# Second scatter: six row transfers a step in the attention instead of four

## The reference

```python
x = x + 0.5 * ffn(layernorm(x), ...)      # mixture of experts
x = x + attn(layernorm(x), ...)           # causal, 16 heads of 64
x = x + 0.5 * ffn(layernorm(x), ...)      # same weights as the first

def ffn(h):                                # h: tokens x 128
    scores = sigmoid(h @ gate_w.T)         # 64 experts, 8 groups of 8
    # the 4 best groups stay, of their experts the 8 best; weights normalised, times 2.5
    y = sum over experts e of w_dense[:, e] * ((silu(h @ Wg[e]) * (h @ Wu[e])) @ Wd[e])
    return y + (silu(h @ Ws_gate) * (h @ Ws_up)) @ Ws_down
```

## Time and profile before

| | us |
|---|---|
| median of 3 runs | 1654.45 (1654.39 to 1654.9) |
| profiled execution, its own time | 1653.0 |
| span of the profile, first to last instruction | 1651.3 |
| TensorE (PE) busy | 1571.9 (95%) |
| VectorE (DVE) busy | 1199.7 (73%) |
| ScalarE (ACT) busy | 776.2 (47%) |
| GpSimd (POOL) busy | 669.7 (41%) |
| POOL L481, both scatters, 256 transfers | 265.3, 1036 ns each |

### The profile page before, as it was taken

One profiled execution on the slowest core, in us unless ns is written; L12 is line 12 of the kernel. 1 busy time (PEld: TensorE's weight loads), 2 busy tenths in 40 slices (PEclk: granted clock), 3 DMA queues, 4 the chain that ended last, 5 costly groups with the idle time before them and its releaser, 6 DMA issues. The chain is left out here.

```text
span 1651.3 us, 27254 instructions
## 1 busy us (share of the span) xinstructions
PE 1571.9 (95%) x8683; PEld 1016.0 (62%) x8683; DVE 1199.7 (73%) x3446; ACT 776.2 (47%) x2105; POOL 669.7 (41%) x931
## 2 busy tenths in 40 slices
PE   5899999998999899999999999998989999999999
PEld 2444444445888677777777776774448986444443
DVE  4698888664555578989898988765866855768675
ACT  2334323222444577777777766773224443222222
POOL 1000288885000334333434105435880003888740
PEclk9999999999999899999999999999999999999999
DMA  9999565563666201000101001104555764666652
GB/s 183 221 261 238 135 148 123 140 144 85 171 190 186 59 22 29 23 22 21 26 20 27 8 4 40 35 25 108 136 129 147 192 189 127 147 147 143 145 131 64
DMA packets 202043, 181.31 MB, mean 110 GB/s; under 512 B 39408, under 2 KB 154288, under 8 KB 201904
## 3 DMA queue, kind: packets, MB, share of 16 engines
q1 hardware_dynamic: 175056, 132.34, 34.0%
q0 software_dynamic: 16384, 33.59, 7.6%
q10 hardware_dynamic: 10464, 13.63, 2.4%
HBM read 121.83 MB, written 57.67 MB: 109 GB/s over the span
## 5 line engine op out<-in xcount | busy, mean ns | idle before, releaser
L840 ACT ACTIVATE f_hid<-banks 128x512 f32<-128x512 f32 (+1 forms) x264 | 157.6, 597 | 506.3 <-PE banks L800 506.2
L481 POOL DMA_INDIRECT x_rows<-r_xk,r_idx x256 | 265.3, 1036 | 137.9 <-issue 53.5
L812 PE MATMUL banks<-f_hid,wd 128*128 128x512 f32 x528 | 273.3, 602 | 11.1 <-DVE f_hid L875 11.1
L862 DVE TENSOR_TENSOR f_hid<-banks,f_hid 128x512 f32<-128x512 f32 (+1 forms) x264 | 181.4, 687 | 139.6 <-ACT f_hid L840 139.2
L796 PE MATMUL banks<-r_xT_d,gu 128*128 128x512 f32 x528 | 275.0, 603 | 4.3 <-DMA wd<-in_L_ffn_We_down 2.7
L800 PE MATMUL banks<-r_xT_d,gu 128*128 128x512 f32 x528 | 272.3, 597 | 0.0
L875 DVE TENSOR_TENSOR f_hid<-f_mix_wide,f_hid 128x512 f32<-128x512 f32 x256 | 175.9, 687 | 32.4 <-DMA f_mix_wide<-mix_rows 30.0
L517 POOL DMA_INDIRECT f_g<-y_rows,r_idx x128 | 129.8, 1014 | 163.3 <-DMA y_rows<-f2q_yq 132.3
L517 POOL DMA_INDIRECT a_g<-y_rows,r_idx x128 | 125.1, 977 | 160.1 <-POOLq L1602 105.1
L812 PEld LDWEIGHTS banks<-f_hid,wd 128*128 128x128 f32 x528 | 99.6, 192 | 144.9 <-issue 119.8
L800 PEld LDWEIGHTS banks<-r_xT_d,gu 128*128 128x128 f32 x528 | 100.6, 191 | 129.2 <-issue 125.2
(11 more groups left out here) (237 smaller groups left out, 2836.4 us busy)
## 6 DMA issues: line engine op xcount, KB each, us to landing
f_mix_wide<-mix_rows SPq DMA_DIRECT2D x124, 512.0 KB, 6.9
x_rows<-zero ACTq DMA_DIRECT2D x12, 1024.0 KB, 6.8
f1q_xq<-x_rows SPq DMA_DIRECT2D x48, 256.0 KB, 3.2
y_rows<-f1q_yq SPq DMA_DIRECT2D x48, 256.0 KB, 2.4
f2q_xq<-x_rows SPq DMA_DIRECT2D x48, 256.0 KB, 3.1
y_rows<-f2q_yq SPq DMA_DIRECT2D x48, 256.0 KB, 2.4
x_rows<-r_xk,r_idx POOLq DMA_INDIRECT x256
wd<-in_L_ffn_We_down SPq DMA_DIRECT2D x7, 512.0 KB, 10.6
```

What stands on the lines that cost most here:

```text
L481: nc.gpsimd.indirect_dma_start(x_rows[:, :], bass.IndirectOffsetOnAxis(ap=b.idx[:, f, CT * k + t, j:j + 1], axis=0), b.xk[:, k, t, :], Non ...
L812: mm = nc.tensor.matmul(acc[:, :], w["wd"][0:rows, 2 * p, :], d.hid[0:rows, g % HIDS, :], start=(p == 0), stop=(p == PAIRS))
L840: nc.scalar.activation(d.hid[0:rows, g % HIDS, :], gate_bank[g % 3][0:rows, :], ACT.Silu)\
L862: nc.vector.tensor_tensor(d.hid[0:rows, g % HIDS, :], up_bank[g % 3][0:rows, :], d.hid[0:rows, g % HIDS, :], ALU.mult).then_inc(gated, 1)
```

## The change

`dispatch` takes a range of single transfers in place of a half tile. In the attention the fifteen steps 49 to 63 issue `SCATTER_STEP` = 6 transfers each in place of 4, so 90 in place of 60. `ffn_second` issues the other 38 in place of 68. There the layer norm operation `rstd_of(in_dense[0])` (L473) stands behind 12 transfers, as before. The order of the transfers and the clears behind those of `ffn_second` are as they were. The first feed-forward block's scatter is written in the new form and has the same instructions.

```diff
-        def dispatch(i, spaced=True):
-            tile, half = divmod(i, 2)
-            k, t = divmod(tile, CT)
-            if t == 0 and half == 0:
-                pool.wait_ge(idx_done, k + 1)
-            for j in HALVES[half]:
+        def dispatch(lists, spaced=True):
+            for i in lists:
+                tile, j = divmod(i, TOPK)
+                k, t = divmod(tile, CT)
+                if t == 0 and j == 0:
+                    pool.wait_ge(idx_done, k + 1)
                 nc.gpsimd.indirect_dma_start(
...
-GATHER_STEP, ADD_LAG = 3, 4
+GATHER_STEP, SCATTER_STEP, ADD_LAG = 3, 6, 4
...
                 if k >= A_DISPATCH:
-                    dispatch(k - A_DISPATCH, spaced=False)
+                    m = SCATTER_STEP * (k - A_DISPATCH)
+                    dispatch(range(m, m + SCATTER_STEP), spaced=False)
...
-                dispatch(i)
+                dispatch(range(4 * i, 4 * i + 4))
...
-            for i in range(dispatched, 2 * SPARSE * CT):
-                if i == dispatched + 3:
-                    rstd_of(in_dense[0])
-                dispatch(i)
+            dispatch(range(dispatched, dispatched + 12))
+            rstd_of(in_dense[0])
+            dispatch(range(dispatched + 12, TOPK * SPARSE * CT))
...
-        ffn_second(nc, w, x_all, psum, b, mix_rows, x_rows, y_rows, second, out_v, tiles // (SEQ // P) * (H // 4) - A_DISPATCH,
+        ffn_second(nc, w, x_all, psum, b, mix_rows, x_rows, y_rows, second, out_v, SCATTER_STEP * (tiles // (SEQ // P) * (H // 4) - A_DISPATCH),
```

## The result

The first four runs of the changed kernel gave 1638.78 us in the median (1638.39 to 1642.34) beside 1654.68 for the kernel before (1654.39 to 1658.79), a ratio of 0.9903, interval 0.9882 to 0.9924. The forecast was 1642.9, its range 1640.5 to 1647.8. Two later trials gave 0.9913 (0.9898 to 0.9928) and 0.9898 (0.9879 to 0.9917). Over all 16 runs of the changed kernel the mean is 1640.6 (1637.4 to 1646.4); over 89 runs of the kernel before on the same chips, one of 4012 us left out, it is 1656.4 (1649.8 to 1661.7). That is 15.8 us, with some 1.4 us either way by the spread of the two. The true gain is above the forecast's 11.6. The mean of all 16 runs lies at the edge of the forecast's range, but the gain lies outside the 14.0 us that the range allowed over 1654.45.

A forecast was written before the change was run, and what follows sets the result against it. Pool's scatter was taken to hold the first quad load, leaving TensorE idle 9.65 us before the quad loop. 11.7 us gained there less 0.1 in the attention made 11.6, so 1654.45 became 1642.85 us, range 1640.5 to 1647.8.

The forecast's parts named there:

- What bounds the kernel, and what is late next: Start of quad loop: scatter holds the first load, TensorE idle 9.65 us; next late are SP's store, then TensorE itself.
- The attention's part: Thirty more transfers in the attention fit Pool's idle time, some 20 us to spare; cost +0.1 us, bounds -1.7 and +2.0.
- The 3.1 us a transfer: Attention, third stretch: by the skill page's port lock, 48 transfers would take 149 us; the prediction weighed this against 1.27 each.
- 11.7 us earlier: Start of quad loop: the step after the first with table rows starts at 1234.30 against 1246.04, no idle time before.
- theory A: From the experiments, not the prediction: TensorE's clock falls or not behind short waits by when they come; 1.7 to 2.2 us each.
- one fall, -1.7 us: Attention: the shift happens to spare the existing clock fall at 1020 to 1025, gaining 1.7 us.
- 44 us earlier: Last stage: with thirty transfers fewer, the scatter is complete by about 1192.3, said to be 44 us earlier.
- late load: Rival, start of quad loop: store and first load hold each other, gain only 6.8 us, 1647.6; chance 8%.
- cost in the attention: Rival, attention: VectorE's delay and one more clock fall cost +2.0 us, 1644.8; chance 7%.
- gap left: Rival, before quad loop: something other than the scatter holds the first load, the gap stays, 1654.4; chance 2%.
- Pool is late out of the attention: Rival, attention's end: slower transfers in a run of 48 make Pool end 24 us late, 1666.8; chance 3%.

The follow-up runs named there:

- e2: Against the kernel before: 90 transfers in the attention, then 68 in the last stage (38 real, 30 to a table nobody reads); 0.9993 of before.
- h4: Against the kernel before, four transfers a step: the second dense chunk's mixing-weight transposes three slots later in the last stage's first dense chunk; 0.9994 of before.
- its control: The kernel before, unchanged, run as if it were a new one; 1.0005 of before.
- e3: Against the kernel before: 60 transfers in the attention, 38 in the last stage, the last 30 never made; 0.9901 of before, median 1640.66 us.
- e4: Against the kernel before: five transfers a step, so 75 in the attention and 53 in the last stage; 0.9915 of before.
- f2: Against the kernel before: ten added 128x512 matmuls behind quad entry 3's step, in the gap before the quad loop; 0.9974 of before.

## Why the prediction fell short, point by point

- **What bounds the kernel, and what is late next: right.** The scatter held the first load and SP's store was next. The load came 0.42 us behind the store (0.4 forecast), L574 5.62 us behind the store (1231.52 - 1225.89 = 5.63 forecast), the following step 2.79 us later (2.78).
- **The attention's part: right.** The layer norm operations kept 2.48 and 3.98 us of waiting (2 and 5.7 forecast), Pool 20.38 us (20). Its cost was put at +0.1; e2, which does this part alone, is 0.9993 of before (0.9983 to 1.0003). The 3.1 us a transfer weighed there, after "SBUF — State Buffer" in the Trainium skill, was not seen: 48 transfers in a row kept 1.27 us each. The prediction applied the page too widely: it ties the lock to some VectorE operations, such as those in a two-port mode, and whether such ones stood beside the transfers no run shows. VectorE did feel something: in the changed kernel single L1459 operations beside the transfers took up to 0.55 us, and at most 0.35 behind them.
- **The term that was mis-sized: "11.7 us earlier".** It was taken from TensorE's times in one profile, and two parts of it hang on the clock. First, the half clock behind the gap: I took its 2.0 us, where three profiles with the gap have 2.0, 2.1 and 3.8, and the kernel kept busy in the gap gained 4.3 (2.3 to 6.5). Second, the start of the comparison: I took the store of the changed kernel to come 94.3 us behind Pool's first transfer, with the fall near 1190 in it. In the kernel before this fall cost nothing, since it lay under the scatter (h4). In the changed kernel dense chunk 0 is the path, and took 92.1, 91.8 and 91.8 us in its three profiles, without the fall. The forecast had counted the chunk with its fall on the new path; this is the step that failed, and it is worth some 2.2 to 2.5 us. From Pool's first transfer to the end of the quad loop the three profiles with the gap have 252.7, 252.1 and 253.7 us, the three of the changed kernel 238.7, 238.4 and 238.4: 14.3 us where the forecast had 11.7.
- **The rest: the attention,** 144.3 us against 143.0, 143.3 and 143.3. The 1.1 us are a fall near 1020. It was in the profiles of before and of its control, and in e3 and e4, but not in the other two with four a step (f2, h4), and in none of ten with six. One thing in the clock's records sorts all eighteen profiles. The clock also fell near 980, ahead of this scatter's first transfer: in the four profiles with the fall near 1020 that fall began 7.90 to 8.26 us before the transfer, in the fourteen without it 8.32 to 9.34 us before. So what goes with the fall near 1020 was there before any of these transfers was issued, which speaks for the moment (theory A) and against the transfers. It is a correlation with a narrow margin, and why all profiles with six a step lie on the side without the fall stays open. With it the profiles make 15.4 us, and the times 15.8 with 1.4 either way.
- **The range** used one fall, -1.7 us, as its lower bound. Several places where the clock may fall lie on this path: near 1020 and 1190, behind the gap, and near 1380, where six of the eighteen profiles have a fall that makes the last three chunks 1.7 us longer (268.7 in place of 267.0). The time of the changed kernel spreads over 9 us (1637.4 to 1646.4). That the first four runs had 1638.8 where all sixteen average 1640.6 is chance, and part of the distance from the range.
- **A slip that changed nothing:** the scatter was said to be complete 44 us earlier; by the rows named there it is 1236.06 - 1190.0 = 46.
- **The base.** The three runs shown had 1654.45; over 89 runs the mean is 1656.4.
- **The rivals.** None of them came: no late load, no cost in the attention, no gap left. "Pool is late out of the attention" is what eight a step does, at 1.0030; my test for it was a slower pace, but the pace held except for one pause, and the number of transfers decided.

## What to carry to other kernels

Where one engine's queue ends a stage, what TensorE loses before that end costs nothing; when the queue is taken off the path, those losses come back into the sum, so count the new path from its own start, with and without each fall of the clock. A gap costs its length and the half clock behind it, and the second part must be read from several profiles. Work moved into idle time must leave some of that time over: six transfers a step left Pool 20 us and gained 15.8 us, seven gave some 8 of them back though Pool was done 5.5 us before TensorE, and eight lost 5 against before.

## What the runs showed of the hardware

TensorE's granted clock fell to the lower of its two levels (1.2 of 2.4 GHz) behind waits of the same length, 2.79 to 2.81 us, in some profiles and not in others. In the changed kernel it fell with the work 0.86 or 1.72 us later, and did not with the work 2.58 us later or not moved. Stretches of the kernel before and of the changed kernel's third trial, busy shares and clock as in the earlier trace rows:

```profile
1188.00:1198.00 10.00, 7.78 (x16) 3.53 (x17) 8.68 (x17) 1.57 (x3) 8.82 (x13) 0.83 0.62 150
```

```profile
1188.00:1198.00 10.00, 7.20 (x20) 3.10 (x19) 9.79 (x22) 2.16 (x4) 4.73 (x8) 1.00 0.53 131
```

The page "TensorE: Matmul & The Clock Gate" of the Trainium skill, section "Part 1: The HAM clock gate", says that the moment at which the clock changes is run-variable, since what watches the activity runs freely and does not start with the kernel. The traces agree: the places below differ between profiles of one and the same kernel.

How long the half clock lasts behind a wait varied more than I had thought: behind 3.3 to 3.4 us of waiting in the first block it took two slow steps in the first profile of the changed kernel, 413.66 - 408.48 = 5.18 and 417.92 - 413.66 = 4.26 us:

```profile
408.48 1.11 PE L574 MATMUL banks<-ident,f1q_xq 128*128 128x128 f32 x4 [3.38 <-DMA f1q_xq<-x_rows]
413.66 1.11 PE L574 MATMUL banks<-ident,f1q_xq 128*128 128x128 f32 x4
417.92 0.66 PE L574 MATMUL banks<-ident,f1q_xq 128*128 128x128 f32 x4
```

The changed kernel's third trial took one slow step there, behind a longer wait:

```profile
408.36 0.90 PE L574 MATMUL banks<-ident,f1q_xq 128*128 128x128 f32 x4 [4.34 <-DMA f1q_xq<-x_rows]
412.74 0.66 PE L574 MATMUL banks<-ident,f1q_xq 128*128 128x128 f32 x4
```

In the kernel before it took one too, of 4.38 us. The 2.3 us between the two first profiles are in code that the change does not touch, and in the difference of the two profiled spans.
